# Router products split off into narrow ones, and a new placement and order for the first sample, in a gated cross-attention and expert kernel

## The reference

```python
# block 1, per sample; h = layernorm(x) over the last axis
t, p, g = Wt @ ctx, Wp @ h, Wg @ ctx                 # 256x256 @ 256x1024
att = sum over group (32 rows x 1024) of p * g       # 8 groups
y = blockdiag(Wz) @ (att * t)
x = x + tanh(g_xattn) * (groupnorm(y) * gn_w + gn_b + ctx)
# block 2, per row; h = layernorm(x)
q = h @ Wq.T                                         # 1024 -> 16
scores = q @ keys.T                                  # 16 -> 64 experts
gate = softmax over the 16 largest scores, 0 elsewhere
z = (h @ A.T) * gate, each gate value for 8 columns  # 1024 -> 512
x = x + tanh(g_ffn) * 2 * (z @ B.T)                  # 512 -> 1024
```

## Time and profile before

| | |
|---|---|
| three timed runs | 377.13, 378.75, 379.71 us (median 378.75) |
| the profiled execution | 377.76 us, its span 376.0 us |
| PE busy | 332.5 us, 88% |
| PEld busy | 304.4 us, 81% |
| DVE busy | 281.3 us, 75% |
| ACT busy | 155.3 us, 41% |
| POOL busy | 146.6 us, 39% |
| mean granted TensorE clock | 0.963 |

### The profile page before, as it was taken

How to read it: one execution, slowest core, us unless ns; L and a number is a source line. 1 busy time by engine, 2 the same in 40 slices (tenths; PEclk the granted TensorE clock), 3 DMA queues, 4 the chain that set the end, 5 groups by cost and what they waited for, 6 DMA issues and landing times.

```text
span 376.0 us, 5690 instructions
## 1 busy us (share of the span) xinstructions
PE 332.5 (88%) x2104; PEld 304.4 (81%) x2104; DVE 281.3 (75%) x674; ACT 155.3 (41%) x253; POOL 146.6 (39%) x98
## 2 busy tenths in 40 slices
PE   2693259809999999999999999999999999999996
PEld 1583159707899988998899889988999889988984
DVE  0888466794886989688968896898869896687342
ACT  1643373433752266135533455417522661135110
POOL 0030051935346615860566254653466058000000
PEclk9999559967999999999999999999999999999999
DMA  7771554355270518123631446062704150001102
GB/s 258 294 224 29 143 210 179 94 177 172 78 260 3 187 50 272 52 83 144 197 140 56 169 130 208 0 224 76 256 6 183 51 197 19 3 1 58 56 28 85
DMA packets 14924, 47.50 MB, mean 126 GB/s; under 512 B 1824, under 2 KB 1952, under 8 KB 14896
## 3 DMA queue, kind: packets, MB, share of 16 engines
q1 hardware_dynamic: 14464, 46.74, 37.0%
q10 hardware_dynamic: 432, 0.40, 0.3%
HBM read 38.74 MB, written 8.39 MB: 125 GB/s over the span
## 4 chain that ended last, share of the span: by engine, by line
PE 77%; DVE 12%; DMA 5%; ACT 3%; issue 2%; POOL 1%; ACTq 0%; SPq 0%; DVEq 0%
PE w_ps L852 24%; PE z_ps L825 22%; PE w_ps L774 11%; PE w_ps L743 9%; PE t_ps L813 3%; PE z_ps L786 3%; DMA raw<-in_cT 2%; DMA norms_sb<-in_norms 2%; DVE B_lo L480 2%; PE t_ps L839 2%; PE w_ps L825 2%; DVE A_lo L480 1%; DVE c_sb L487 1%; PE t_ps L756 1%; DMA uw<-in_aT 1%
## 5 line engine op out<-in xcount | busy, mean ns | idle before, releaser
L257 POOL TENSOR_TENSOR xT_lo<-raw,xT_hi 128x1024 fp32r<-128x1024 f32 x14 | 41.8, 3003 | 34.7 <-ACT xT_hi L327 34.7
L852 PE MATMUL w_ps<-B_hi,zT_hi 128*128 128x512 f32 x128 | 52.7, 411 | 0.0
L852 PE MATMUL w_ps<-B_hi,zT_lo 128*128 128x512 f32 x128 | 50.3, 393 | 0.0
L852 PE MATMUL w_ps<-B_lo,zT_hi 128*128 128x512 f32 x128 | 50.0, 391 | 0.0
L825 PE MATMUL z_ps<-A_hi,hT_hi 128*128 128x288 f32 x224 | 49.0, 301 | 0.0
L825 PE MATMUL z_ps<-A_lo,hT_hi 128*128 128x288 f32 x224 | 48.3, 298 | 0.0
L825 PE MATMUL z_ps<-A_hi,hT_lo 128*128 128x288 f32 x224 | 48.2, 297 | 0.0
L262 POOL TENSOR_TENSOR cT_lo<-raw,cT_hi 128x1024 fp32r<-128x1024 f32 x14 | 33.5, 2395 | 27.9 <-DVE uw L576 16.8
L774 PE MATMUL w_ps<-c_hi,Wu_hi 128*128 128x512 f32 x64 | 27.0, 421 | 14.1 <-DVE M_lo L520 11.0
L743 PE MATMUL w_ps<-cT_hi,xT_hi 128*128 128x256 f32 x128 | 37.1, 290 | 1.0 <-POOL cT_lo L262 0.6
L825 PEld LDWEIGHTS z_ps<-A_hi,hT_hi 128*128 128x128 f32 x224 | 36.8, 191 | 0.5
(11 more groups left out here) (123 smaller groups left out, 795.9 us busy)
## 6 DMA issues: line engine op xcount, KB each, us to landing
c_sb<-in_ctx SPq DMA_DIRECT2D x16, 512.0 KB, 4.1
raw<-in_xT SPq DMA_DIRECT2D x16, 512.0 KB, 5.7
x_sb<-in_x SPq DMA_DIRECT2D x16, 512.0 KB, 3.7
raw<-in_cT SPq DMA_DIRECT2D x14, 512.0 KB, 4.7
out_block<-uw SPq DMA_DIRECT2D x14, 512.0 KB, 2.9
uw<-in_aT SPq DMA_DIRECT2D x8, 256.0 KB, 2.7
uw<-in_bT SPq DMA_DIRECT2D x8, 256.0 KB, 3.3
uw<-in_cT SPq DMA_DIRECT2D x2, 512.0 KB, 9.1
```

Source lines behind the costliest of these rows:

```text
L257: pool.tensor_tensor(xT_lo[:, half_of(h), :], raw[:, half_of(h), :], xT_hi[:, half_of(h), :].bitcast(f32), ALU.subtract).then_inc(xT_lo_s, 1)
L852: last = pe.matmul(w_ps[k][:, :], z[:, t, row], w[:, j, cols], start=(j == 0 and z is zT_hi and w is B_hi), stop=(j == KN - 1 and z is zT_lo))
```

## The change

1. **The router.** A keeps 512 columns. The product Wq^T·keys^T goes, with its copy and rest. Wq is instead loaded transposed, 128 x 8 x 16, and split into `Wq_hl` (16 hi and 16 lo columns per k). Per k, `z_product` has three products of 512 columns into one bank, and beside them one of 32 columns (`Wq_hl` under `hT_hi`) and one of 16 (its hi part under `hT_lo`) into the other. New steps follow: `gate` scales the 32 columns to `q_sb` (DVE); PE transposes it (`scores`, step 0); ACT copies it to `qT_sb`; PE multiplies it with the keys, which are stacked twice and so add the hi and lo parts (step 1), a plain float32 product; DVE copies the 64 scores to `sc`. The two PE steps are put into the product that follows `z_product(t, b)`: after the products of k = 1 and k = 3 of `gram`, or after those of the first two inner steps of `z_product`, `u_product` or `out_product`. `zg_sb` is then written by one instruction of 512 columns, not two of 288.
2. **Raw lots.** The 16 lots have 16 entries in a list of places: quarters of `raw`, quarters of `uw1` and the two halves of `stage`. The transposed ctx of sample 1 goes to `uw1`. The waits of the SP queue follow.
3. **Order of the first sample.** `wt` is the first transfer of SP; tanh comes behind the first splits on ACT; DVE takes the statistics of x ahead of those of u; `x_plus_ctx` of sample 0 is done by POOL in four instructions (`x_plus_ctx_first`), no longer by DVE; `gram(0)` has banks of its own (`z_ps`) and so doesn't wait for `u_copy(0)`; ACT does the first four lots ahead of `M_high(0)`, `w_square(0)` behind `hT_high`, and `cT_high(0, 1)` ahead of the scores. `w_square` writes its unused output to other tiles.

```diff
@@ places of the lots
-        def slot(j):
-            return flat1[:, (j % SLOTS) * HALF:(j % SLOTS + 1) * HALF]
+        quarters = [raw[:, 2 * i:2 * i + 2, :].rearrange("p k c -> p (k c)") for i in range(4)]
+        quarters1 = [flat1[:, i * HALF:(i + 1) * HALF] for i in range(4)]
+        halves = [stage[:, i * HALF:(i + 1) * HALF] for i in range(2)]
+        slots = quarters + quarters1[2:4] + halves + quarters + quarters1[0:2] + halves
+
+        def z_banks(t, n):
+            return w_ps[NH:USES] if t == 1 and n in (0, NB - 1) else z_ps
+
+        def gram_bank(n, t):
+            return z_ps[t] if n == 0 else w_ps[t]
@@ SP, order of the first sample
+            sp.dma_start(wt_nat, wt).then_inc(wt_in, 16)
             load_c(0)
...
-            for j in range(SLOTS):
+            for j in range(KD - 2):
+                load_lot(j)
+            load_cT(0, 1)
+            for j in range(KD - 2, KD):
                 load_lot(j)
             load_xT(1)
-            for j in range(SLOTS, KD):
-                load_lot(j)
             load_x(1)
             load_c(1)
-            for j in range(KD, KD + KN):
+            load_cT(1, 1)
+            for j in range(N_LOTS - 2, N_LOTS):
                 load_lot(j)
-            load_cT(1)
-            for j in range(KD + KN, N_LOTS):
+            for j in range(KD, N_LOTS - 2):
                 load_lot(j)
@@ POOL
+            def x_plus_ctx_first():
+                pool.wait_ge(beta_done, 1)
+                pool.wait_ge(c_lo_s, T)
+                for t in range(T):
+                    step(pool.tensor_scalar(c_sb[:, t, :], c_sb[:, t, :], tg[:, 0:1], beta[:, t:t + 1],
+                                            ALU.mult, ALU.add))
+                for t in range(T):
+                    settle()
+                    pool.tensor_tensor(c_sb[:, t, :], c_sb[:, t, :], x_sb[:, t, :], ALU.add).then_inc(xt_done, 1)
@@ ACT
             def exps(t, n):
+                act.wait_ge(qT_done, per_tile(n, t))
+                act.activation(qT_sb[:, :], z_banks(t, n)[1][0:QC, P:2 * P], ACT.Copy).then_inc(qT_s, 1)
                 act.wait_ge(max_done, per_tile(n, t))
...
-            u_copy(0)
             cb_copy(0)
...
-            act.wait_ge(router_done, 1)
-            act.activation(A_hi[:, :, NN:ZC], ...)
+            u_copy(0)
+            for j in range(KN):
+                lot_high(j)
             M_high(0)
-            for j in range(KD):
+            for j in range(KN, KD):
                 lot_high(j)
             for h in range(NH):
                 xT_high(h, 1)
-            w_square(0)
             hT_high(0, 0)
             hT_high(1, 0)
+            w_square(0)
@@ DVE
-                step(dve.tensor_scalar(sc[:, :], banks[1][:, ZH - NE:ZH], w_rs[:, t:t + 1], None, ALU.mult))
+                dve.tensor_scalar(q_sb[:, :], banks[1][:, 0:QC], w_rs[:, t:t + 1], None, ALU.mult).then_inc(q_s, 1)
+                dve.wait_ge(scores_done, per_tile(n, t))
+                step(dve.tensor_copy(sc[:, :], banks[1][:, 2 * P:2 * P + NE]))
...
-            u_statistics(0)
             x_stats(0)
...
+            u_statistics(0)
...
-            x_plus_ctx(0)
+            lot_low(0)
+            lot_low(1)
             gram_fix(0)
@@ PE
-                    for h, w in ((hT_hi, A_hi), (hT_hi, A_lo), (hT_lo, A_hi)):
-                        for i in range(2):
-                            last = pe.matmul(banks[i][:, 0:ZH], h[:, t, row], w[:, k, i * ZH:(i + 1) * ZH],
...
+                    pe.matmul(banks[0][:, :], hT_hi[:, t, row], A_hi[:, k, :], start=first, stop=False)
+                    pe.matmul(banks[1][:, 0:QC], hT_hi[:, t, row], Wq_hl[:, k, :], start=first, stop=False)
+                    pe.matmul(banks[0][:, :], hT_hi[:, t, row], A_lo[:, k, :], start=False, stop=False)
+                    pe.matmul(banks[1][:, 0:RD], hT_lo[:, t, row], Wq_hl[:, k, 0:RD], start=False, stop=last_k)
+                    last = pe.matmul(banks[0][:, :], hT_lo[:, t, row], A_hi[:, k, :], start=False, stop=last_k)
+                    if k < 2:
+                        query(k)
...
+            def scores(t, n):
+                bank = z_banks(t, n)[1]
+                def query(step):
+                    if step == 0:
+                        pe.wait_ge(q_s, per_tile(n, t))
+                        pe.transpose(bank[0:QC, P:2 * P], q_sb[:, :], ident[:, :]).then_inc(qT_done, 1)
+                    else:
+                        pe.wait_ge(qT_s, per_tile(n, t))
+                        pe.matmul(bank[:, 2 * P:2 * P + NE], qT_sb[:, :], keys_sb[:, :], start=True,
+                                  stop=True).then_inc(scores_done, 1)
+                return query
...
-                    z_product(1, b, w_ps[NH:USES])
+                    z_product(1, b, scores(0, b))
                     zT(0, b)
-                    gram(m, lambda: ctx_sums(m))
+                    gram(m, lambda: ctx_sums(m), scores(1, b))
+                    u_product(m)
                 else:
-                    gram(m, lambda: ctx_sums(m))
+                    gram(m, lambda: ctx_sums(m), scores(0, b))
                     zT(0, b)
                     z_product(1, b)
-                u_product(m)
+                    u_product(m, scores(1, b))
```

More of the change, by code:

```diff
@@ L186, in load_lot @@
             def load_lot(j):
[L187 to L191, removed]
+                if j < 4:
+                    sp.wait_ge(xT_lo_s, per_tile(0, j // 2))
+                elif j < 6:
+                    sp.wait_ge(cT_lo_s, per_tile(0, 1))
+                elif KD <= j < 12:
+                    sp.wait_ge(xT_lo_s, per_tile(1, (j - 8) // 2))
+                elif 12 <= j < 14:
+                    sp.wait_ge(cT_lo_s, per_tile(1, 0))
+                elif j >= 14:
+                    sp.wait_ge(lot_lo_s, KD)
                 if j < KD:
@@ L400, in lot_high @@
                 act.activation(lot_dest(j)[0], slot(j), ACT.Copy).then_inc(lot_hi_s, 1)
[L402 to L403 removed]
+            c_high(0, 0)
             act.wait_ge(wu_done, 1)
@@ L410, in _ @@
                 cT_high(h, 0)
-            u_copy(0)
+            act.wait_ge(norms_in, 16)
+            act.activation(tg[:, :], norms_sb[:, 0:2], ACT.Tanh).then_inc(tanh_done, 1)
+            act.wait_ge(wq_in, 16)
+            act.activation(Wq_hl[:, :, 0:RD], Wq_sb[:, :, :], ACT.Copy).then_inc(wq_hi_s, 1)
             cb_copy(0)
@@ L432, in _ @@
                 if b == 0:
-                    for h in range(NH):
-                        cT_high(h, m)
+                    cT_high(1, m)
                     residual(b)
@@ L730, in _, with gram @@
         def _(pe):
-            def gram(n, between):
+            def gram(n, between=lambda: None, query=lambda step: None):
                 for t in range(T):
-                    if n == 0:
-                        pe.wait_ge(u_copied, per_use(n, t))
-                    elif n >= 2:
+                    if n >= 2:
                         pe.wait_ge(out_added, per_use(n - 2, t))
@@ L758, in ctx_sums, with u_product @@
                 last.then_inc(cb_done, 1)
-            def u_product(n):
+            def u_product(n, query=lambda step: None):
                 if n > 0:
@@ L814, in hT, with z_product @@
                     last.then_inc(hT_done, 1)
-            def z_product(t, n, banks=z_ps, gated=None):
+            def z_product(t, n, query=lambda step: None, gated=None):
+                banks = z_banks(t, n)
                 for k in range(KD):
@@ L822, in z_product @@
                     row = slice(k * P, k * P + P)
-                    for h, w in ((hT_hi, A_hi), (hT_hi, A_lo), (hT_lo, A_hi)):
-                        for i in range(2):
-                            last = pe.matmul(banks[i][:, 0:ZH], h[:, t, row], w[:, k, i * ZH:(i + 1) * ZH],
-                                             start=(k == 0 and h is hT_hi and w is A_hi),
-                                             stop=(k == KD - 1 and h is hT_lo))
+                    first, last_k = k == 0, k == KD - 1
+                    pe.matmul(banks[0][:, :], hT_hi[:, t, row], A_hi[:, k, :], start=first, stop=False)
[5 more added lines that the diff above has]
+                        query(k)
                     if gated and k == KD - 3:
@@ L840, in zT, with out_product @@
                 last.then_inc(zT_done, 1)
-            def out_product(k, n, middle=None):
+            def out_product(k, n, middle=None, query=lambda step: None):
                 t, cols = use(k)
@@ L869, in _ @@
             u_product(0)
-            def router():
-                ctx_sums(0)
-                pe.wait_ge(wq_in, 16)
-                pe.wait_ge(keys_in, 16)
-                for k in range(KD):
-                    last = pe.matmul(z_ps[1][:, k * NE:k * NE + NE], wq_sb[:, k * P:k * P + P], keys_sb,
-                                     start=True, stop=True)
-                last.then_inc(router_done, 1)
-            gram(0, router)
+            ctx_sums(0)
+            gram(0)
```

(4 more changed lines are left out.)

136 lines of the change are left out of this document (72 added, 64 removed).

## The result

The changed kernel takes 403.34 us (median of 4 runs, 402.51 to 404.25), beside 379.23 for the kernel before in the same series (377.13 to 380.95): a ratio of 1.064, with a 95% interval of 1.058 to 1.070. It is slower, as forecast, but by 24 us where 16 were forecast, and just above the range. The profiled execution took 402.51 us with a span of 400.7, against 377.76 and 376.0; the spans differ by 24.7.

The account below looks back on a forecast made before the run. PE's stream was taken to bound the loop, a chain through DVE, ACT and transfers the start. Loop and last sample +22.4 us, start -6, sum +16.4: 394.2 us profiled, 394.5 as a median; range 383 to 402.

Parts of the forecast that it names:

- The narrow product: On PE in `z_product`: each of the 16 narrow products costs 0.113 us, the tile +0.88 us.
- Rival A: On PE: a narrow product is cheap, 0.03 us each, so the kernel gets faster, 374 us; chance 0.12.
- The wide product: On PE: 24 products of 512 columns per `z_product` at 0.2275 us each, within a `z_product` of 7.27 us.
- The scores step: New on PE in each tile: transpose of the query and product with the keys, together +0.34 us.
- The keys term: On PE, within the scores step: the plain float32 product with the keys is two instructions at 0.113 us each.
- The stall in `group_means`: In each sample's period: PE stops about 0.75 us for DVE's longer gate 1 and statistics; bounds 0 to 1.5.
- The start: First pass, ahead of the loop: `u_product(1)` starts at about 79.3, a gain of 6 us; bounds -3 to -10.
- 1. `n_product(0)`: Start, step 1: DVE waits 0.8 for tanh but loses `x_plus_ctx`; net -1.2 us, from 32.54 to 31.3.
- 2. `hT_hi`: Start, step 2: on ACT, xT(1) is issued earlier and squares stand behind; -7.2 us, from 49.76 to 42.5.
- 3. The lots of B: Start, step 3: through `z_product(0, 0)`, tile 0's gate and ACT's splits, to 61.1 from 68.04; -6.9 us.
- 4. The four lots: Start, step 4: lots take 5.58 us on DVE, gate 1 5.5, then 7.33 to `u_product(1)` at about 79.3.
- Rival C: First pass: the start gives nothing, as gate 1 waits for PE and ACT and holds up DVE; 400 us, chance 0.12.

Follow-up runs that it names:

- narrow_left_out: Changed kernel with 12 of the 16 narrow products of each `z_product` left out, for its time alone: 382.8 us, ratio 1.012 to the kernel before.
- narrow_112: Changed kernel with both narrow products widened by zero columns to 112 columns, from 32 and 16: 402.25 us, ratio 1.063 to the kernel before.
- keys_32_moved: Changed kernel with the buffer sizes and addresses of keys_128, but 32 weight rows in the keys product: 401.77 us, ratio 1.062 to the kernel before.
- keys_128: Changed kernel with the query tile zero-padded, so the keys product has 128 weight rows instead of 32: 398.74 us, ratio 1.056 to the kernel before.
- folded_query: Changed kernel with the query columns folded into two 264-column halves of A, no narrow products, keys product with 128 rows: 378.25 us, ratio 0.999.
- early_M: order_only with the first sample's x + ctx on VectorE and its M ahead of all lots: 367.91 us, ratio 0.972 to the kernel before.
- order_only: Changed kernel with the old folded router, so the new placement and order alone: 373.71 us, ratio 0.989 to the kernel before.

## Why the prediction was right in its sign and short in its size

**The narrow product: right.** 0.113 us was taken from the earlier trace rows; narrow_left_out measures 0.113 in the loop, and narrow_112 shows that columns up to 112 are free there. Rival A (0.03) is refuted. So is what the Trainium skill's figure for 1 to 64 columns, which it gives for an isolated product, would have given here (TensorE: Matmul & The Clock Gate, "Back-to-back issue gap"): by it the kernel would be at 373; the measurement decides.

**The wide product: nearly right.** `z_product` came to 7.37 for 7.27. The missing 0.1 is 24 times 4 ns: in the changed kernel two 512-column products in a dense stretch start about 232 ns apart, not the 0.2275 us of the earlier trace rows. With other addresses, in keys_32_moved, the dense stretches are at 227 again and a `z_product` at 7.31, so 0.06 of the 0.1 are back.

**The scores step: mechanism right, size half.** The keys term, "plain float32, so two instructions, at 0.113 each", was taken from products with 128 weight rows. With 32 rows it costs about 0.33 more in a tile, shown by keys_128 and keys_32_moved. That is 0.66 in a sample and some 4.6 us of PE's time over the loop and last sample.

**The stall in `group_means`: 0.1 for 0.75.** I had PE back after 7.7 us and VectorE after 8.4 to 8.5, counted from the end of `z_product(1, b)`. In the trace, PE is back at 137.38, after 8.10, and VectorE about as early. The dearer keys product, and 512-column products somewhat slower, filled most of the slack that I had seen as a stall; the rest is a gate somewhat faster than counted. In keys_128, where the keys product costs what I had counted, `group_means` takes 0.38, a stop of 0.26; in folded_query the chain does run through VectorE. So this term and the last erred in opposite directions, and the period came out at 43.6 for 43.2.

**The start: the step that failed.** The forecast was `u_product(1)` at 79.3, "-6". It came at 86.17, a miss of 6.9 us. Of these, 1.7 came back, as `u_product(1)` took 5.86 instead of 7.55, and 0.2 were lost again behind it. (The numbered steps add up to 79.5, not 79.3; 0.2 of the miss are that slip.) Of the 8.3 us by which the difference of spans is off (24.7 for 16.4), 5.5 are here and 2.8 in the loop and the last sample. By its numbered steps, all in the chain of the changed kernel:

```profile
26.23 2.36 DVE Wp_lo L714
...
33.98 2.91 PE z_ps L828 x12
...
40.75 5.33 DMA raw<-in_xT
...
46.16 1.06 ACT xT_hi L360
47.22 0.49 ACT hT_hi L416
```

1. `n_product(0)` at 33.98, not 31.3. I had the two lots at 0.62 each, the price "when POOL is idle", and moved x + ctx to GpSimd, beside them, in the same step without asking what that does to them: 2.83 for the first, and 2.44 for the split of Wp. `n_product` then also ran at the lower granted clock, 2.91 us against 1.67. PE had stood for 7.5 us ahead of it, and for 2.9 before the change.
2. `hT_hi` at 47.22, not 42.5. Step 1 carries on; xT(1) is issued at 40.4 rather than 36.5, and its landing, through 46.1, ends what ScalarE waits for. ScalarE has it ahead of `hT_hi` in its queue. early_M turns that around.
3. The lots of B at 66.58, not 61.1. Of the 5.5, 4.7 come from steps 1 and 2; as a stretch, from `hT_hi` on, this step was nearly right, 19.4 us for 18.6.
4. The four lots took 6.82 (I had 5.58, bounds down to 2.48, none above). Gate 1 took the 5.5 that I gave it, 73.33 to 78.8, and the rest was right too.

So the miss of 6.9 is made of steps 1 and 2 (4.7), a somewhat dearer step 3 (0.8), the lots of B (1.2) and the slip. Put by cause, the -6 was a sum of two parts. One was the router. From the start of `z_product(0, 0)` to ScalarE's exp of gate 0 the forecast has 11.9 us (45.5 to 57.4) where the kernel before takes 8.5 (52.7 to 61.20), so 3.4 more, and it has 1.3 more for gate 1, 4.7 in all. (The changed kernel takes 12.5.) These are the rows of exp, before and after; `z_product(0, 0)` starts at 52.7 and at 50.2:

```profile
61.20 0.35 ACT L392 ACTIVATE ex<-sc,neg_max 128x64 f32<-128x64 f32 x1 [5.43 <-DVE neg_max L604]
```

```profile
62.64 0.35 ACT L431 ACTIVATE ex<-sc,neg_max 128x64 f32<-128x64 f32 x1 [1.72 <-DVE neg_max L650]
```

The other part was the placement and order, which by the same count must then have been some -10.6. order_only measured them at -5.0, and the router costs 6.0 between order_only and the changed kernel. **The placement fell short by 5.6, the router was 1.3 dearer than counted: that is the 6.9.** Where the placement did work is the load of `cT(1)`: before, ScalarE stands for it (7.92 us from 56.34), and in order_only the stretch from `hT_hi` to the lots of B takes 15.1 us (47.52 to 62.57) against 18.3. The clock then gives 2.5 of the router's 6.0 back, so at the loop's start the change as a whole gained 0.54.

Rival C named the size (the start gives nothing, 400), and at 0.12 it was held too cheap. But its cause isn't what the runs show: gate 1 with its waits took the 5.5 us that the forecast gave it, and the time was lost ahead of it. That the time lies near C's 400, with the dearer keys product on top, is in part luck.

## What to carry to other kernels

A matrix product that loads its own weights had a floor of one weight load here, 0.11 us: splitting 64 columns off a pair of products into two narrow ones of their own is a loss, even with fewer columns in all, and folding the 16 query columns back into the wide ones takes 20 to 22 us off (from keys_128 to folded_query). Price a new round trip between engines apart for each stretch of the program, by the engine that bounds that stretch: the wait for the scores lay beneath PE in the loop, and in the first pass two of them cost over 4 us on VectorE's chain. Ask of every operation handed to GpSimd what VectorE does in that moment; and put what a chain waits for ahead of bulk work in every queue: early_M, whose edits do that and weren't timed apart, took another 6 us off, where the placement had taken 4.

## What the runs showed of the hardware that was not expected

- A product with 32 weight rows between products with 128 makes TensorE run empty on both sides: 0.32 and 0.36 us between weight loads where 0.12 and 0.22 are usual, about 0.33 in all. Zeros up to 128 rows remove it. (32 rows and 128 are the two cases that ran.)
- In dense stretches the 512-column products started about 232 ns apart in the changed kernel and 227 in keys_32_moved, which differs from it only in buffer sizes and addresses (5.69 against 5.57 us for a stretch of 24 with its edges). Which address matters wasn't tried.
- GpSimd's operations on 128 x 1024 elements beside VectorE's splits of 128 x 512 slow the latter from 0.68 to 2.44 and 2.83 us.
- An earlier start behind a longer stand of PE was worth a fifth of itself: 2.06 us at `u_product(1)` became 0.45, as the 24 products took 7.46 instead of 5.86 at the granted clock that they found.
